# The written orders of five engines in a two-block cross-attention kernel, dealt anew

## What is computed

```python
def _L1_xattn_ref(query, key, value, Wq, bq, Wk, bk, Wv, bv, Wo, bo):
    q = _split_heads(query @ Wq.T + bq, B, Q)
    k = _split_heads(key @ Wk.T + bk, B, KV)
    v = _split_heads(value @ Wv.T + bv, B, KV)
    scores = jnp.einsum('bhqd,bhkd->bhqk', q, k) / SCALE
    top_scores, top_idx = jax.lax.top_k(scores, 32)
    w = jax.nn.softmax(top_scores, axis=-1)
    ...
x = x + jnp.tanh(g_xattn[0]) * _L0_xattn_ref(_layernorm(x), ctx_1024, ctx_1024, ...)
x = x + jnp.tanh(g_ffn[0])   * _L0_ffn_ref(_layernorm(x), ...)      # 8 experts, the best 2
x = x + jnp.tanh(g_xattn[1]) * _L1_xattn_ref(_layernorm(x), ctx_1024, ctx_1024, ...)
x = x + jnp.tanh(g_ffn[1])   * _L1_ffn_ref(_layernorm(x), ...)      # self-attention and 8 experts
```

## Time and profile before

| | |
|---|---|
| median of 3 runs | 5390.07 us (5384.35 to 5394.43) |
| span of the profiled execution | 5390.7 us |
| PE busy in it | 4654.8 us, 86% |
| DVE busy | 4315.2 us, 80% |
| ACT busy | 4029.9 us, 75% |
| POOL busy | 1153.0 us, 21% |

### The profile page before, as it was taken

One profiled execution on the slowest core, in us unless ns is written; L12 is line 12 of the kernel. 1 busy time (PEld: TensorE's weight loads), 2 busy tenths in 40 slices (PEclk: granted clock), 3 DMA queues, 4 the chain that ended last, 5 costly groups with the idle time before them and its releaser, 6 DMA issues. The chain is left out here.

```text
span 5390.7 us, 109932 instructions
## 1 busy us (share of the span) xinstructions
PE 4654.8 (86%) x34502; PEld 2211.0 (41%) x34502; DVE 4315.2 (80%) x22968; ACT 4029.9 (75%) x5196; POOL 1153.0 (21%) x2648
## 2 busy tenths in 40 slices
PE   4878779999797999889899999997999799988776
PEld 2435235353443535344353534444353444534222
DVE  4457887879888797987988798898879888877772
ACT  1447767879687787868778797886879688886763
POOL 2121112222121222212222222222222122121110
PEclk7889899999998999999999999999999999999886
DMA  4232222223122232322323232221323122121110
GB/s 122 69 77 55 58 62 60 71 58 82 48 72 62 57 71 60 78 53 63 72 52 75 58 75 61 73 70 49 75 56 81 49 64 67 48 57 28 34 24 19
DMA packets 356330, 332.18 MB, mean 62 GB/s; under 512 B 102073, under 2 KB 313148, under 8 KB 355710
## 3 DMA queue, kind: packets, MB, share of 16 engines
q1 hardware_dynamic: 355710, 324.84, 24.8%
HBM read 217.54 MB, written 107.13 MB: 60 GB/s over the span
## 5 line engine op out<-in xcount | busy, mean ns | idle before, releaser
L951 DVE MAX8 cand<-s 128x8 f32<-128x67 f32 (+1 forms) x12288 | 1998.7, 225 | 117.5 <-ACT s L903 68.9
L922 ACT ACTIVATE prob<-wide 128x1024 f32<-128x1024 f32 (+1 forms) x1792 | 1775.3, 1025 | 379.9 <-PE wide L644 181.9
L1037 DVE TENSOR_REDUCE part<-score 128x1 f32<-128x512 f32 x1536 | 1031.8, 683 | 346.7 <-PE score L598 247.6
L690 PE MATMUL att<-prob,v 128*9 128x256 f32 (+1 forms) x14336 | 1104.5, 388 | 27.6 <-ACT prob L922 25.9
L644 PE MATMUL wide<-q,k_att 128*128 128x256 bf16 (+1 forms) x6656 | 1014.3, 279 | 101.5 <-ACT s L903 53.9
L903 ACT ACTIVATE s<-wide 128x1024 f32<-128x1024 f32 (+1 forms) x1024 | 844.4, 846 | 286.2 <-DVEq L1094 149.5
L912 ACT ACTIVATE below<-wide 128x1024 bf16<-128x1024 f32 (+1 forms) x832 | 828.7, 1024 | 131.3 <-PE wide L644 122.6
L644 PEld LDWEIGHTS wide<-q,k_att 128*128 128x128 bf16 (+1 forms) x6656 | 580.8, 100 | 564.7 <-ACT s L903 148.7
L598 PE MATMUL score<-k_scan,q 128*128 128x512 bf16 x1536 | 584.1, 396 | 176.2 <-DVE part L1037 86.0
L1283 POOL TENSOR_SCALAR flag<-cand,ends 128x24 bf16<-128x24 f32 x512 | 177.5, 347 | 2461.7 <-DVE ends L976 2254.9
L666 PE MATMUL wide<-below,minus_ident 128*128 128x512 bf16 (+1 forms) x1664 | 504.5, 386 | 101.8 <-ACT below L912 90.9
(11 more groups left out here) (164 smaller groups left out, 5335.4 us busy)
## 6 DMA issues: line engine op xcount, KB each, us to landing
k_scan<-k_stack SPq DMA_DIRECT2D x512, 150.1 KB, 2.7
k_stack<-split_b SPq DMA_DIRECT2D x576, 128.0 KB, 2.5
k_att<-k_stack SPq DMA_DIRECT2D x384, 192.0 KB, 3.4
ctxT<-in_ctx_dram SPq DMA_DIRECT2D x32, 800.5 KB, 5.6
q_stack<-split_b SPq DMA_DIRECT2D x192, 64.0 KB, 2.1
q<-q_stack SPq DMA_DIRECT2D x128, 96.0 KB
self_stack<-split_b SPq DMA_DIRECT2D x192, 64.0 KB, 2.2
k_self<-self_stack SPq DMA_DIRECT2D x64, 96.0 KB
```

Source lines behind the costliest of these rows:

```text
L690: r = tensor.matmul(att[32 * j:32 * j + HD + 1, 0:S], v[0:kc, c, j0 * HG + j, :], m.prob[n % 3][0:kc, j * S:(j + 1) * S], start=(c == 0), ...
L922: scalar.activation(pr[0:kc, :], ps[0:kc, :], ACT.Exp, scale=SCALE).then_inc(sem["wide_done"], 1)
L951: i = vector.max(cand[:, :, c], s[:, KCUT[c]:KCUT[c + 1]])
L1037: vector.tensor_reduce(m.part[:, QT * hh + qt, c:c + 1], score[i % 2][:, :], AX.X, ALU.max).then_inc(sem["score_max"], 1)
```

## The change

The strings of PE, ACT, DVE and SP are written anew, with the lags of their words; POOL's string is only broken over lines in another way, and its lags stay. No instruction, buffer, wait rule or tile is edited, and each word stands in its turn as often as before. The turn now begins at another place of the batch, which alone would make most words look moved; for example:

```diff
     pe={
-        "cut_add": 216, "c1": 244, "pv.1": 217, "n0": 223, "row_turn.0": 9, "s_1": 215, "w_k.1": 9, "flag": 62,
+        "cut_add": 148, "c1": 160, "pv.1": 150, "n0": 79, "row_turn.0": 3, "s_1": 147, "w_k.1": 4, "flag": 42,
     dve={
-        "rank": 491, "n0_max": 225, "n0_all": 9, "check": 62, "o_norm.1": 17, "least": 16, "x_add.1": 5,
+        "rank": 310, "n0_max": 72, "n0_all": 3, "check": 40, "o_norm.1": 12, "least": 10, "x_add.1": 3,
```

More of the change, by code:

```diff
@@ new lines @@
+        s_1 pv.1 cut_add pv.1 flag cut_add w_k.0 c1 z_score n0 c1 v_w1 z_score*2 pv.1 v_w1 n0 s_1 v_w2 s_1 n0
+        cut_add v_w2 cut_add z_score c1 n0 flag c1 n0 s_1 row_turn.2 c1 pv.1 cut_add row_turn.1 pv.1*2 v_w1 n0 v_w1
+        pv.1 n0*2 c1 v_w2 c1 s_0 n0 v_w2 c1 s_0 pv.0 flag s_0 n0*2 w_v.0 s_0 pv.0 n0 s_0 n0 v_w1 u_turn.1 n0 v_w1
+        ln_turn.w pv.0*2 n0 s_0 v_w2 s_0 c1 n0 pv.0*2 n0 s_0 w_k.0 s_0 pv.0 n0 s_0 w_q pv.0*2 s_0 n0 c1 v_w2 s_0
+        v_w1 n0 v_w1 flag pv.0*3 c1 v_w2 s_0 s_z n0 v_w2 s_z z_score pv.0 s_1*2 pv_z*2 cut_add u_turn.0 z_score*2
@@ new lines @@
+    dve="""
+        ln_stats.w v_add rank ln_aggr.w n0_max rank v_add n0_max ln_scale.w rank n0_max*3 check n0_max rank n0_max
+        o_norm.1 rank n0_max rank n0_max v_add n0_max rank*4 n0_max*2 v_add check v_add n0_max*2 rank*2 z_max v_add
+        x_add.v ln_stats.u ln_aggr.u o_norm.0 z_max*3 rank n0_max o_norm.2 n0_max rank ln_scale.u n0_all z_max
+        n0_max rank*3 z_max n0_max rank n0_max rank n0_max*2 rank z_max check n0_max*2 rank n0_max z_max rank*3
+        n0_max rank n0_max rank n0_max*2 rank n0_max rank check n0_max least n0_max rank*2 n0_max rank*2 n0_max
+        o_norm.1 rank o_norm.2 rank*2 n0_max*2 rank check rank n0_max rank n0_max rank n0_max*2 rank*2 n0_max rank
+        z_max*2 o_norm.0 rank check n0_max o_norm.2 rank z_max*2 rank n0_max*2 rank n0_max rank*2 n0_all n0_max rank
+        n0_max*2 rank n0_max rank n0_max rank check rank n0_max rank n0_max*3 rank n0_max rank n0_max*2 rank*2
+        n0_max rank check rank least o_norm.1 rank n0_max*2 rank n0_max rank*3 o_norm.2 n0_max*2 rank*2 check n0_max
+        rank*3 n0_max*2 rank n0_max o_norm.0 n0_max rank n0_max rank x_add.z n0_max rank*2 n0_max rank n0_max check
+        n0_max rank n0_all rank n0_max rank n0_max rank*2 n0_max rank n0_max*3 rank*2 n0_max check n0_max*2 rank*2
+        n0_max rank*4 n0_max rank o_norm.1 rank n0_max check rank n0_max least rank n0_max rank n0_max*2 rank
+        x_add.1 rank ln_stats.z ln_aggr.z n0_max rank ln_scale.z n0_max rank*3 n0_max check n0_max rank n0_max*2
+        o_norm.0 rank n0_max rank n0_max rank*2 route_best.z n0_max*2 rank x_add.0 rank ln_stats.v ln_aggr.v
+        n0_max*2 check ln_scale.v n0_all route_pick.z rank*2 n0_max z_add n0_max route_best.v rank n0_max rank*3
+        n0_max rank z_add check n0_max rank z_max n0_max route_pick.v z_max rank*2 z_max rank*2 v_add rank*2
+        n0_max*2 v_add z_max n0_max check n0_max least rank*3 n0_max rank n0_max rank*2""",
@@ L187 @@
     sp={
[3 rows of a table removed]
-        "split_out.u_q": 3, "ctx_in.1": 2, "x_out": 5, "x_in": 0},
[3 rows of a table added]
+        "split_out.u_q": 2, "ctx_in.1": 1, "x_out": 4, "x_in": 0},
 )
```

149 lines of the change are left out of this document (63 added, 86 removed), and 6 rows, old and new, of the table sp.

## The result

The changed kernel takes 5206.24 us (median of four executions, three of them at 5197.62 to 5209.11), the kernel before 5387.21 us beside it. The ratio is 0.9658, with a 95% interval of 0.964 to 0.9675: 3.4% less. The forecast was 5353 us, with a range down to 5285. The direction was right. (The fourth execution was disturbed, with 8281.88 us, and is left out of the ratio.)

What follows compares the result with a forecast made beforehand. PE and ACT, coupled through small rings, were taken to hold the batch in turns, with unhidden repairs on DVE. The sum was 5390.7 - 45 - 24 - 8 + 40 = 5353.7, so 5353 us, range 5285 to 5440.

Steps and rivals of the forecast that it cites:

- Filling and draining at nothing: Start (0 to 881) and end (from 4961) keep the same first and last steps within a few places; costed at nothing.
- SyncE's `x`: Load asked for 32 places later; issued 122 us ahead of use, 39 us left, so costed at nothing.
- Fills closer together, 40 us lost: PE's fills of `wide` with little work since the fill two before rise from 73 to 87: 40 us lost, bounds 0 and 80.
- The joins, 45 us: Weighings in a row on PE: 14 joins in the first block's attention save 0.20 us each, 45 us, bounds 0 and 54.
- `cut_add`, 24 us: More PE work between scores and `cut_add`, so fewer waits for ACT's marks: 24 us saved, bounds 0 and 45.
- The weighings' own waits, 8 us: PE's weighings waited 1.0 us and get a pair of chunks more; half taken, 8 us saved, between 0 and 16.
- Scans and checks at 0: DVE's check stands further behind its `ends`, but PE hardly waits for DVE: 0, between 30 won and 60 lost.
- Repairs unchanged: Eight repairs in `check`, by data the change does not touch; a batch with one still 25 us longer.
- DVE's bunches: Slower rival: runs of three or four `rank` steps hold PE at scans, 56 us; 5454 or 5435 us, chance 0.20.
- The much faster case (5262): Rival: DVE's waits for experts and checks stand in the batch's loop and half goes, some 128 us; chance 0.08.
- The rival in which the saved time is handed to a wait: No change: ACT's passes hold the first block too, so PE's saved time becomes waiting; 5398 us, chance 0.15.
- The rule beside it: Packing speeds up TensorE but not the emptying of PSUM; by it the joins would bring 0 and not 45.

Runs made afterwards that it cites:

- b_join: Kernel before, with the first weighing moved behind a single c1 fill standing between two weighings, 134 joins more: 5413.23 us, ratio 1.0045.
- a_part: Changed kernel, with two adjacent weighings parted by the c1 fill or n0 scan behind them, 171 times: 5235.37 us.
- a_join: Changed kernel, with the first weighing moved behind a single c1, n0, s_0 or s_1 between two weighings, 69 joins more: 5215.18 us, ratio 0.9669 to before.
- b_dve: Kernel before without repairs, with VectorE's first-layer maxima taken over 128 of 512 columns: 5158.80 us, 301.3 us a batch.
- the mixed order at 3400: One stretch of a five-order kernel: kernel before with TensorE's small steps and ScalarE's copies for them changed; batch 11 took 356 us, before 301.
- pv_new: Kernel before, with TensorE's weighings moved to their places in the changed order (47 moves): 5605.01 us, ratio 1.0397.

## Why the prediction was wrong

*Filling and draining at nothing: the step that failed most.* "Keep the same first and last steps within a few places" was true of the lists and did not bear the conclusion. These stretches hold 90 of the 189 us, 50 and 40, where the forecast itself named 10 us as a sign of being wrong. The earlier trace rows had the sign of it: in the first 881 us PE is busy for 676.6 only, and such a stretch has room for waits that places decide. The forecast looked at SyncE's `x` alone and put its other loads, which "mostly stand earlier", at nothing. SyncE's list was worth 25 us.

*Fills closer together, 40 us lost: wrong sign.* The kernel was expected to lose 2.5 us a batch there. By the ends of its steps the times before `c1`, `w_k`, `w_v` and `s_z` fell by some 4.4 us a batch and those before `s_1` and `s_0` rose by 2.2. The mechanism is real, as `b_join` shows at 0.26 us a fill. But it counted PE's work between two fills as if ScalarE stood still, and in the changed kernel ScalarE's drains were moved too, by up to six places. That this is why the sign turned is argued and not shown: no run changed ScalarE's list alone. The term was also worked out wrong in its own numbers: 11.0 us and 28 waits of 0.16 more are 15.5 and not 13, so it would have been 48 us and not 40.

*The joins, 45 us: right in size, and in part by luck.* 0.20 us was forecast for each. With 16 fewer runs of weighings a batch (1639 to 1382 over the run) the weighings' steps have 3.1 to 3.5 us less, some 0.2 each and 34 to 39 us over eleven steady batches; by the price in `a_part`, 0.27, it would be 47. The forecast counted batches of the fill that pay nothing, and took one price for all joins, which `b_join` and `a_join` did not bear out.

*`cut_add`, 24 us: right.* PE's wait fell from 4.5 to 3.3 us a batch, by the ends of steps from 8.3 to 6.2: 19 to 34 us over 16 batches, inside the bounds.

*The weighings' own waits, 8 us: right.* 1.0 us fell to 0.5, one wait in each of the two batches shown.

*Scans and checks at 0: nearly right for the steady batch.* PE's wait for the maxima stayed under 1 us, and a lighter VectorE gave the kernel before nothing; yet by the ends of steps PE's scans have 1.9 us a batch less, for a reason that is open. It was wrong in the fill, where the lighter VectorE brought `w_q` 4 from 834 to 796 us and the difference of the two orders from 54 to 38.

*Repairs unchanged: in number, not in price.* Eight, as said. They are worth 191 and 184 us by the totals, 200 and 181 by the spans. In the trace a batch with one is 22 us longer after (315 against 293), 25 before, which makes 22 us over the six steady ones that the forecast put at nothing. The clock column moves with it: 0.95 in the earlier trace rows, 0.97 after.

*The rivals.* DVE's bunches did not come: PE's wait for the maxima is 0.6 us. The much faster case (5262) was nearest in its number and wrong in its reason, as `b_dve` shows. The rival in which the saved time is handed to a wait put the joins at nothing, and `a_part` measured 29 us for 171 of them. The rule beside it, of the Trainium skill ("TensorEngine Tiling (Array Packing)", "PSUM Bottleneck"), says that the emptying of PSUM may become the limit; the trace agrees in part, since ScalarE held PE before `cut_add` (2.1 us a batch of the gain) and not in the weighings. The steady forecast without the closer fills would have been 77/16 = 4.8 us a batch, of a measured 7.1; the larger part of the miss is the fill and the end.

The account of the 189 us: fill 50 (SyncE's list 25, the rest open, VectorE being part of it), end 40 (about half of it hangs on ScalarE's weight), steady 99. Of the steady part 78 is the batch itself (7.1 x 11, a batch: weighings 3.1, `cut_add` 2.1, scans 1.9 and fills 1.8 less, small steps 1.7 more), and the rest are its six repairs, which cost 21.7 us each and not 25.3.

## What to carry to other kernels

Price the stretches where the busiest engine waits, the fill and the end, before the steady loop: a new order acts there through loads and through engines that hold little later. Compare two orders at the same count of steps, and not at a step that has itself moved. When a rewritten order moves two coupled engines together, do not price one list's distances against the other's old times. To find who holds a loop, do not mix two tuned orders; take work off one engine in both kernels and see which time moves, since a large wait on an engine with slack follows the loop and does not make it.

## What the hardware showed unasked

More waiting on PE can go with a lower clock. In the mixed order at 3400 the granted clock is 0.92 and PE is busy 307 us for work that takes 280 at 1.00, so there a stall was paid about twice. It does not always: the batch of `pv_new` at 3206 is 15 us longer than before at a granted clock of 0.99. In the fill 0.88 became 0.90 with the shorter waits. And a VectorE reduction over 128 columns took 286 ns where 512 columns take 682, a ScalarE pass over 256 columns 384 ns where 1024 take 1025: by a straight line through the two points about 150 and 170 ns of them do not depend on the width, an estimate.
